# Turns of the identity in the head of an attention and expert kernel, and the last units' work in pieces between the first expert blocks

## The reference

```python
# x: 16 x 256 x 128, ctx: 16 x 1601 x 128, mask: 16 x 1601
h = layernorm(x)
Q, K, V = h @ Wq + bq, ctx @ Wk + bk, ctx @ Wv + bv
s = where(mask == 0, -1e9, Q @ K.T / sqrt(128))
x = x + softmax(s) @ V

h = layernorm(x)
xn = rms_norm(h, norm_scale)
top, ids = top_k(xn @ w_router.T, 2)          # 8 experts, 2 for each token
w = softmax(top)
up = xn @ w_up[ids].T                         # 2 x 256 columns
u, gate = split(up, 2)
y = (u * silu(gate)) @ w_down[ids].T
x = x + h + sum over the 2 choices of w * y
```

## Time and profile before

| | us |
|---|---|
| median of 3 runs | 409.93 |
| lowest, highest | 409.09, 411.86 |
| the profiled execution | 408.3 |
| its span, first to last instruction | 406.5 |
| busy in it: PE, DVE, ACT, POOL | 369.1, 320.8, 272.9, 221.3 |
| mean granted clock of PE | 0.965 of full |

### The profile page before, as it was taken

The page is one execution under the profiler, slowest core; times in us unless marked ns, Lnnn a source line. Parts: engine busy times, 40 slices in busy tenths (PEclk is TensorE's granted clock), DMA queues, the critical chain, the costliest instruction groups (busy, mean ns, idle before and its releaser), DMA issues.

```text
span 406.5 us, 9976 instructions
## 1 busy us (share of the span) xinstructions
PE 369.1 (91%) x2608; PEld 341.3 (84%) x2608; DVE 320.8 (79%) x1354; ACT 272.9 (67%) x646; POOL 221.3 (54%) x377
## 2 busy tenths in 40 slices
PE   3589999999999999999999999787997999999950
PEld 2489999999999999999999999676875788888840
DVE  4777889889889899889889899556675777777785
ACT  3156877867867867867867866546774677887740
POOL 6012232575575575565565574337777656666570
PEclk9979999999999999999999999799999999999995
DMA  6873574484584584584484560301222543333677
GB/s 211 251 263 111 192 266 126 176 280 135 191 276 141 187 284 137 185 294 127 183 297 131 179 187 22 91 15 54 73 87 81 125 102 85 85 99 91 216 279 239
DMA packets 57846, 66.65 MB, mean 164 GB/s; under 512 B 5920, under 2 KB 49200, under 8 KB 57792
## 3 DMA queue, kind: packets, MB, share of 16 engines
q1 hardware_dynamic: 51520, 55.15, 42.7%
q0 software_dynamic: 4320, 8.92, 6.6%
q10 hardware_dynamic: 1952, 1.94, 1.4%
HBM read 53.88 MB, written 12.11 MB: 162 GB/s over the span
## 4 chain that ended last, share of the span: by engine, by line
PE 78%; POOL 8%; issue 6%; DVE 4%; DMA 3%; ACT 1%; POOLq 0%; SPq 0%; ACTq 0%
PE ps L1416 24%; PE ps L1381 17%; PE ps L1398 12%; PE ps L1569 9%; PE ps L1597 5%; POOL rows_in L578 3%; POOL parts L651 3%; PE ps L1586 3%; PE ps L1367 2%; PE ps L1542 2%; PE ps L1443 2%; DVE base_all L1318 1%; DVE attention L1312 1%; DMA attention<-parts 1%; PE ps L1436 1%
## 5 line engine op out<-in xcount | busy, mean ns | idle before, releaser
L1416 PE MATMUL ps<-attention,ctx_sb 128*128 128x128 f32 (+1 forms) x832 | 107.6, 278 | 0.0
L1416 PEld LDWEIGHTS ps<-attention,ctx_sb 128*128 128x128 f32 (+1 forms) x832 | 99.0, 192 | 0.0
L651 POOL DMA_INDIRECT parts<-mbias,blk_x x71 | 70.2, 988 | 33.3 <-ACT mbias L845 23.9
L578 POOL DMA_INDIRECT rows_in<-kept,place x64 | 72.6, 1135 | 17.5 <-issue 17.5
L724 ACT ACTIVATE attention<-ps 128x512 f32<-128x512 f32 x96 | 55.6, 596 | 20.8 <-PE ps L1398 20.8
L1398 PE MATMUL ps<-ident,attention 128*128 128x128 f32 (+1 forms) x416 | 65.3, 280 | 0.0
L930 DVE CUSTOM_DVE_ANT_0 attention<-ps,mbias 128x1608 f32<-128x1608 f32 x32 | 58.5, 1828 | 7.9 <-issue 7.2
L709 ACT ACTIVATE attention<-attention,ebias 128x1601 f32<-128x1601 f32 x32 | 52.4, 1636 | 17.9 <-DVE ebias L948 17.7
L545 POOL TENSOR_TENSOR rstd<-ve,minus_half 128x2 f32<-128x2 f32 x32 | 22.9, 715 | 75.9 <-DVE ve L991 75.9
L1381 PE MATMUL ps<-ctxt_high,gt_high 128*128 128x402 f32 x128 | 51.0, 398 | 5.2 <-DVE ctxt_low L1048 3.0
L1398 PEld LDWEIGHTS ps<-ident,attention 128*128 128x128 f32 (+1 forms) x416 | 52.4, 145 | 3.5 <-ACT attention L724 0.4
(11 more groups left out here) (162 smaller groups left out, 789.8 us busy)
## 6 DMA issues: line engine op xcount, KB each, us to landing
ctxt_in<-ctx_cols SPq DMA_DIRECT2D x16, 800.5 KB
ctx_sb<-ctx_rows SPq DMA_DIRECT2D x16, 768.0 KB
mbias<-mbias_dram SPq DMA_DIRECT2D x15, 800.5 KB, 5.6
blk_x<-rows_in SPq DMA_DIRECT2D x71, 65.0 KB, 1.9
attention<-parts SPq DMA_DIRECT2D x6, 512.0 KB, 4.9
x_in<-x SPq DMA_DIRECT2D x16, 128.0 KB, 2.1
wup_in<-w_up_t SPq DMA_DIRECT2D x8, 256.0 KB
out<-base_all ACTq DMA_DIRECT2D x6, 256.0 KB, 2.4
```

Of the source, the lines that this page charges most:

```text
L578: pool.indirect_dma_start(rows_in, bass.IndirectOffsetOnAxis(ap=place[:, c, u:u + 1], axis=0), kept[:, u % KEPT, c], None).then_inc(s_scat ...
L651: pool.indirect_dma_start(parts, bass.IndirectOffsetOnAxis(ap=blk_x[:, m % XR, D:D + 1].bitcast(I32), axis=0), blk_y[:, m % YR], None).the ...
L1416: last = pe.matmul(ps_o[:, 0:P], ctx_sb[0:n, j, t], probs_t[0:n, t * P:(t + 1) * P], start=t == 0, stop=t == KT - 1)
```

## The change

Three things. PE turns the identity 14 times before it waits for the constants and 12 times before the first scores; nothing reads what it writes. In the head DVE norms batch 1 ahead of the maximum of unit 0, ACT makes the high part of batch 1's columns ahead of the first exp, and POOL clears its filler rows after its tables rather than before them. At the end of the attention, slots 32 and 33 are taken apart: their instructions stand in a function `late(m)` on PE, DVE and ACT, after steps 1 to 10; POOL's last eight scatters stand one before every third result, from result 8 on; and block 1 is turned into bank 1 rather than bank 0, so that it needn't wait for block 0.

```diff
         def run(eng, slot, before_steps, step, late):
             ...
             for m in range(NB + 3):
                 step(m)
-                if m in LATE_SLOTS:
-                    u = UNITS - 1 + LATE_SLOTS.index(m)
-                    slot(u // 4, u % 4)
+                if m == 0:
+                    slot(PAIRS - 1, 3)
+                late(m)
@@ POOL
-            pool.memset(filler[:], 0.0).then_inc(s_filler, 1)
             pool.memset(ones[:], 1.0).then_inc(s_tables, 1)
             ...
             pool.tensor_copy(before_r[:], before[:]).then_inc(s_tables, 1)
+            pool.memset(filler[:], 0.0).then_inc(s_filler, 1)
             rstd_of_x(0, 1)
             ...
-            for u, m in enumerate(LATE_SLOTS):
-                if m < 3:
-                    slot(UNITS - 1 + u)
+            slot(UNITS - 1)
+            slot(UNITS)
             for m in range(NB):
-                if m + 3 in LATE_SLOTS:
-                    slot(UNITS - 1 + LATE_SLOTS.index(m + 3))
-                if m + 2 == LATE_SLOTS[3]:
-                    for n in range(TOP_K + 1):
-                        scatter(TOP_K * (UNITS - 4) + 1 + n)
-                if m == LAST_RANK:
-                    for n in range(2 * TOP_K):
-                        scatter(TOP_K * (UNITS - 2) + n)
+                if m == 3:
+                    slot(UNITS + 1)
+                if m == 7:
+                    count_batch(B - 1)
+                    name_results(B - 1)
+                n = m - 8
+                if n >= 0 and n % 3 == 0 and n // 3 < 4 * TOP_K:
+                    scatter(TOP_K * (UNITS - 4) + n // 3)
                 send_result(m)
@@ ACT
+            split_ctxt(0, 1)
             exp_unit(0, 0)
-            split_ctxt(0, 1)
             ...
+            def late(m):
+                if m == 1:
+                    norm_unit(UNITS - 2)
+                if m == 2:
+                    copy_turned_row(UNITS - 2)
+                    add_skip(UNITS - 2)
+                if m == 3:
+                    norm_unit(UNITS - 1)
+                if m == 5:
+                    second_gate(UNITS - 2)
+                    copy_turned_row(UNITS - 1)
+                    add_skip(UNITS - 1)
+                if m == 8:
+                    second_gate(UNITS - 1)
@@ DVE
             query_bias(0, 0)
+            ln1(0, 1)
             dve.wait_ge(s_mfirst, 1)
             maximum(0, 0)
             bias_sum(0, 0)
             bias(0, 0)
-            ln1(0, 1)
             ...
+            def late(m):
+                i = PAIRS - 1
+                if m == 1:
+                    post_sum(i, 3)
+                    ...
+                    gates_second(i, 1)
+                if m in (4, 7):
+                    k = 2 + (m - 4) // 3
+                    best(i, k)
+                    best_index(i, k)
+                    best_difference(i, k)
+                    best_number(i, k)
+                if m in (6, 9):
+                    k = 2 + (m - 6) // 3
+                    gates_sum(i, k)
+                    gates_hot(i, k)
+                    gates_first(i, k)
+                    gates_second(i, k)
+                if m == 10:
+                    find_places(B - 2)
@@ PE
+            def warm_up(turns):
+                for n in range(turns):
+                    pe.transpose(ps_turn[:, 1, 0:P], ident[:], ident[:])
+
+            pe.wait_ge(s_ident, 1)
+            warm_up(14)
             pe.wait_ge(s_consts_qk, N_CONSTS)
             ...
             prep_gt(0, 0)
+            warm_up(12)
             score(0, 0, range(SCORE_CHUNKS))
             ...
-                wait(pe, s_xt_low, m)
-                pe.transpose(ps[:, 0, 0:P], blk_x[:, m % XR, 0:D], ident[:]).then_inc(s_bxt, 1)
+                if m > 1:
+                    pe.wait_ge(s_xt_low, 1 if m == 2 else m)
+                pe.transpose(ps[:, rows_bank(m), 0:P], blk_x[:, m % XR, 0:D], ident[:]).then_inc(s_bxt, 1)
             ...
+            def late(m):
+                if m == 1:
+                    attend(UNITS - 1)
+                if m in (2, 5):
+                    turn_row(UNITS - 2 + (m - 2) // 3)
+                if m in (3, 6):
+                    route(PAIRS - 1, 2 + (m - 3) // 3)
+                if m == 9:
+                    rank_batch(B - 2)
```

More of the change, by code:

```diff
@@ L88, in xattn_moe @@
     CH = 4
-    LATE_SLOTS = [0, 2, 6, 9]
     LAST_RANK = 12
@@ L363, in is_unit, with rows_bank, run @@
             return not isinstance(u, int) or 0 <= u < UNITS
+        def rows_bank(m):
+            return 1 if m == 1 else 0
         def is_block(m):
             return not isinstance(m, int) or 0 <= m < NB
-        def run(eng, slot, before_steps, step):
+        def run(eng, slot, before_steps, step, late):
             for u in range(UNITS - 1):
@@ L609, in _ @@
             pool.memset(begins[:], 0.0).then_inc(s_tables, 1)
-            pool.wait_ge(s_filler, 1)
-            pool.iota(filler[:, :, D].bitcast(I32), pattern=[[P, FILLS]], base=TOP_K * TOK,
-                      channel_multiplier=1).then_inc(s_filler, 1)
             pool.wait_ge(s_tables, 8)
@@ L622, in _ @@
             pool.tensor_copy(before_r[:], before[:]).then_inc(s_tables, 1)
+            pool.memset(filler[:], 0.0).then_inc(s_filler, 1)
             rstd_of_x(0, 1)
+            pool.wait_ge(s_filler, 1)
+            pool.iota(filler[:, :, D].bitcast(I32), pattern=[[P, FILLS]], base=TOP_K * TOK,
+                      channel_multiplier=1).then_inc(s_filler, 1)
             pool.wait_ge(s_consts, N_CONSTS)
@@ L636, in slot @@
                         name_results(b - 2)
-                    if b >= 3 and u != 2 * B + 2:
+                    if b >= 3:
                         scatter(4 * (b - 3) + 1)
@@ L817, in block_xt @@
                 wait(act, s_up, m - AHEAD)
-                act.activation(xt_high[:, m % (AHEAD + 1)], ps[:, 0, 0:P], ACT.Copy).then_inc(s_xt_high, 1)
+                act.activation(xt_high[:, m % (AHEAD + 1)], ps[:, rows_bank(m), 0:P], ACT.Copy).then_inc(s_xt_high, 1)
             def before_steps():
@@ L846, in step @@
                                    scale=blk_x[:, n % XR, D + 1:D + 2]).then_inc(s_y2, 1)
-            run(act, slot, before_steps, step)
+            def late(m):
[12 more added lines that the diff above has]
+                    second_gate(UNITS - 1)
+            run(act, slot, before_steps, step, late)
             for n in range(FIRST_CHUNKS):
@@ L1301, in split_block @@
                 wait(dve, s_up, m - AHEAD)
-                dve.tensor_tensor(xt_low[:, m % (AHEAD + 1)], ps[:, 0, 0:P], xt_high[:, m % (AHEAD + 1)].bitcast(F32),
+                dve.tensor_tensor(xt_low[:, m % (AHEAD + 1)], ps[:, rows_bank(m), 0:P], xt_high[:, m % (AHEAD + 1)].bitcast(F32),
                                   ALU.subtract).then_inc(s_xt_low, 1)
@@ L1339, in before_steps @@
                     split_block(m)
-            run(dve, slot, before_steps, step)
+            def late(m):
+                i = PAIRS - 1
+                if m == 1:
+                    post_sum(i, 3)
+                    post(i, 3)
+                    gates_sum(i, 1)
+                    ln2_stats(i, 3)
+                    gates_hot(i, 1)
+                    ln2_moments(i, 3)
+                    gates_first(i, 1)
+                    ln2_var(i, 3)
+                    gates_second(i, 1)
[13 more added lines that the diff above has]
+                    find_places(B - 2)
+            run(dve, slot, before_steps, step, late)
             for n in range(2 * len(CHUNKS)):
@@ L1347, in _ @@
         def _(pe):
+            def warm_up(turns):
[3 more added lines that the diff above has]
+            warm_up(14)
             pe.wait_ge(s_consts_qk, N_CONSTS)
             pe.wait_ge(s_pad, 3)
-            pe.wait_ge(s_ident, 1)
             def prep_xt(i, j):
@@ L1613, in before_steps @@
                     turn_block(m)
-            run(pe, slot, before_steps, step)
+            def late(m):
[7 more added lines that the diff above has]
+                    rank_batch(B - 2)
+            run(pe, slot, before_steps, step, late)
 def kernel(x, ctx_1024, mask_BxS2_ik0, L0_xattn_Wq, L0_xattn_bq, L0_xattn_Wk, L0_xattn_bk, L0_xattn_Wv,
```

## The result

| | before | after |
|---|---|---|
| median, four runs each | 409.85 | 399.36 |
| lowest, highest | 409.09, 411.86 | 398.17, 400.02 |
| the profiled execution, its span | 408.3, 406.5 | 399.84, 398.0 |
| mean granted clock of PE | 0.965 | 0.966 |

The ratio is 0.9729 with a 95% interval of 0.9694 to 0.9763. The kernel is 10.5 us faster; predicted were 402.3 and a range of 397.5 to 407.5. The two profiled executions differ by 8.5; the other 2.0 lie in how far each of them stood from its median.

The account below looks back on a forecast made before the run. PE was taken as the bound, nearly always busy, so other engines' time counts only where PE waits. Gains summing to 7.6 took the profiled 408.3 to 400.7; with the median 1.6 higher, 402.3, range 397.5 to 407.5.

Parts of the forecast that it names:

- head: Start of the kernel: norm of batch 1 ahead of the maximum gains 1.0, earlier full clock 0.9; together 1.9 (0.5 to 3.5).
- bank of block 1: Before step 0: PE no longer waits for block 0's low part, one round of three goes; gain 1.2 (1.0 to 1.4).
- clock at the first blocks: At the first blocks: the clock probably falls again but returns a little sooner; gain 0.5 (0 to 2.4).
- pieces: Steps 1 to 15: slots taken apart leave stalls of 6.6 where they were 7.4; gain 0.8 (loss 3.4 to gain 2.5).
- scatters: Steps 15 to 30: spread scatters remove PE's wait for block rows, excess 5.1 for 8.3; gain 3.2 (2 to 5).
- rival 3: No clock fall at the first blocks (1.6), pieces cost DVE's share alone (1.7), head 0.8 more; 398.2, chance 0.12.
- rival 4: Block phase: ten stalls make the clock drop near step 3 and stay down to step 15; +12.8, 415, chance 0.03.
- Rival 1: In the head: turns of the identity don't wake the clock, so the head gains 1.3; 402.9, chance 0.08.
- after about 17.3: In the head: ACT's copy of batch 1's columns delays the exp only if the columns land later than about 17.3.

## Why the prediction was right, term by term

| term | predicted | between the profiles | median with that part undone |
|---|---|---|---|
| head | 1.9 | 2.1 | 0.8 (1.7 at the first block) |
| bank of block 1 | 1.2 | 1.2 | 1.4 (with the clock) |
| clock at the first blocks | 0.5 | 1.3 | |
| pieces | 0.8 | 1.4 | 2.8 |
| scatters | 3.2 | 3.6 | 4.3 |
| behind step 30 | 0 | -1.05 | |
| sum | 7.6 | 8.5 | |

**Scatters and bank**: right in mechanism and size. No PE wait for block rows is left near step 22, and POOL has not become the bound. The four table passes cost 0.86, 0.91, 0.85 and 0.74 where 0.9 each was predicted (steps of 2.35, 2.40, 2.34 and 2.23 against 1.49). One part of the scatters' price had no name in the prediction: of the 3.6, the hole itself is 2.45 (the step took 4.80, now 2.35), and 0.9 lies in the three steps behind it, where the clock stood at one half from 313.1 to 316.5. And only one of the two table passes stood inside the hole (308.06); the second came behind it (314.57).

**Pieces**: right in sign, too small. Steps 1 to 15 hold 14 undisturbed steps of 1.49, 20.9, and an excess estimated at 6.6. Where the clock held they take 25.55, an excess of 4.7, so the pieces are worth 2.7. The term that was sized wrong is most likely ACT's: 1.5 for norms, "the others give 0.5 each", while in the profile after PE has no wait of over 0.15 for ACT in these steps. The first of DVE's pieces came through as priced: it stretched step 3 to 2.85, 1.36 above a quiet step, for its 1.48. How the other 3.3 divide between DVE's later pieces and PE's own extra work, no run separates. Priced by DVE alone, 3.6 with overlap, and with 0.7 for the last places the sum would have been 4.3. That was rival 3's half.

**Clock among the blocks**: half right. That it would fall again at the first blocks did not come true in the changed kernel's profile; instead it fell at step 3, the place that rival 4 named, and returned after 3.4, not at step 15. So what step 0 gained by it (1.3) steps 1 to 15 lost again (26.90 against 25.55): the clock brought nothing in all and the pieces the whole 2.7. Had it stayed up in both stretches the two terms would have brought 4.0 where 1.3 was predicted, so part of the agreement of the sum is luck. A fall costs 0.7 to 1.5 here (7.8 against 7.1 in step 0; 2.93 against 1.66 from step 3 to step 4; two steps with whole slots 4.56 against 3.04 before). It happens in ten of the fourteen profiles at four places: the first blocks, step 3, step 7, and right behind a long wait for block rows. At the first two, twins with the same code up to that place differ. That term belongs to the execution as much as to the kernel, and 0.5 with a range of 0 to 2.4 was as much as the trace of before could give.

**Head**: right in its sum, wrong in one of its steps and in two readings. By landmarks the first turns of probabilities came 1.55 earlier (22.00 to 20.45) where 1.0 was predicted, and the earlier grant made it 2.3 by the next unit's first turns (31.28 to 28.94), 0.8 more where 0.9 was predicted. The readings: 22.21 was had by adding a duration, 0.69, where the distance is 0.48; and PE was not at the lower level all the while, since the scores of the next unit stood 0.19 apart from 18.84 to 19.40, not 0.335:

```profile
18.84 0.35 PE L1381 MATMUL ps<-ctxt_low,gt_high 128*128 128x402 f32 x1
19.03 0.35 PE L1381 MATMUL ps<-ctxt_high,gt_low 128*128 128x402 f32 x1
22.00 1.06 PE L1398 MATMUL ps<-ident,attention 128*128 128x128 f32 x4
```

The step: "If they lift the clock, scores end two microseconds earlier, which alone is worth nothing: the maximum that follows is held by DVE." DVE holds it only because the change put the norm of batch 1 ahead of it. With the old order the maximum followed the scores at once, 14.01, and the turns alone gave what both give, at the first block 1.2 more. The two edits compete: the order fills an idle stretch that exists while the scores run at half clock, and the turns remove that stretch. With the clock up from the scores on, the order costs 1.1 to 2.1 on the way to the first block. I priced each edit against the trace of before and added them. ACT's copy of the columns held the exp besides, 18.54 against a bias that was ready at 18.18, as the prediction's condition ("after about 17.3") came close to saying.

**Rival 1, by the rule**: it falls. In the kernel with the old order PE had done nothing but 14 turns before 5.05, and its first product pair ran in 0.51 rather than 0.80; in the head of 53 turns the clock held through every stretch that the turns filled. The Trainium skill, "TensorE: Matmul & The Clock Gate", Part 4 (PE-mode transpose), says that transposes do not engage the full rate. The trace does not agree.

**Behind step 30**: nothing was predicted, and 1.05 was lost. From POOL's issue of the last result to the first sum of it on DVE 6.4 passed instead of 5.8 (385.64 to 392.08; 394.78 to 400.62 before), so 0.6 is a transfer that took longer at the end; the 0.4 of steps 30 to 70 is spread over many steps. I did not look for its cause.

The median moved 2.0 more than the profiles: before's profiled run lay 1.55 below its median, after's 0.5 above.

## What to carry to other kernels

Price two edits of one stretch together: when one fills an idle time and the other removes its cause, the gains do not add, and the pair can be worse than the better half (399.7 for 53 turns with the new order, 396.4 for the same turns with the old). Where PE is the bound but idles on data, cheap work in its idle stretches kept its clock here; a gap left open can give it away again (2.01 ahead of the scores in the changed kernel, then a fall at 12.9), but need not (1.69 at the same place with the old order, and none there). A piece of 0.9 on the engine that feeds the bound cost about its length, one of 0.5 often less; ACT's pieces, on an engine with slack, made no wait of PE that shows.

## What the runs showed of the hardware that was not expected

The same 14 turns raise the clock at different times: at 5.05 the first product pair already ran in 0.49 and 0.51 in two profiles, while in three others the second group of turns still ran at half rate (12 in 2.40, 16 in 2.89 and 2.97), and the scores behind it began up to 1.0 later (12.35 against 11.34, with the same code up to there). The landing of the columns moves it too: ACT began their copy at 7.79 and at 8.41 in two kernels with the same head, and the scores began at 11.34 and 11.97. So the head varies by about one from one execution to the next.

A fall of the clock in the block phase lasted 3.4 in each of the nine profiles after the change that have one, 6.8 and 3.4 before it. Its place wanders between the first blocks and step 7; the two falls further on (313.1 before, 308.0 with grouped scatters) both stand right behind a wait of PE for block rows.
